# First matrix product of batches 4 to 15: a seven-product scheme replaced by three passes over 12-bit parts, with a direct projection

## The chip, the cores and the metric

One core of one Trainium2 chip runs the kernel. The metric is the device time of one execution in microseconds, the median over the runs made. The kernel before takes 173.54 us (three runs, 172.73 to 173.70).

## The reference

```python
# x (16, 256, 512), cond (16, 256), W3 (256, 512), W2 (512, 512), weight and rram (512, 512), all float32
q_emb = relu(cond @ W3 + b3)                           # (16, 512)
v_sum = sum(x, axis=1, keepdims=True)
h = relu(((256 * x + v_sum) * q_emb[:, None, :]) @ W2 + b2)
x_q = where(h > 0.33, 0.5, where(h < -0.33, -0.5, 0.0))
w_q = where(weight > 0.2, 0.6, where(weight < -0.2, -0.6, 0.0))
return x + einsum('bsd,od->bso', x_q, w_q + rram)
```

The first product ends in a comparison: of `h` only the side of 0.33 on which it lies is kept. The second product (the projection) takes 0 or 1 for each hidden value and a factor 0.5 at the end. The 16 batches of 256 tokens make 4096 tokens, 32 output tiles of 128 tokens by 512 columns.

## The kernel before, in words

Each engine has a list of operations written out by hand, and semaphores order the engines. Nothing is moved by a scheduler: an engine works through its list in order, and an operation behind a waiting one waits too.

Input: SyncE loads x two batches (a "pair") at a time into two slots of `x_in`. VectorE transposes a batch into `xT` in one instruction (`transpose_batch`, L532). The token sum of a batch comes from VectorE (L581, batches 2, 3, 6, 7) or from ScalarE (`accumulate`, L436), and ScalarE scales the batch in four pieces of 128x256 (`scale`, L430). Batches 0 and 1 are handled in finer pieces at the start.

First product: batches 0 to 3 are multiplied directly in float32 by `w2_sb` (L1005, L1010, L1018). Batches 4 to 15 are three groups of four batches. A group is a 2x2 block product of 512-token halves and 256-row halves of W2, done with seven block products instead of eight (`p1` to `p7`, L855 to L927). VectorE makes four sums of x blocks for it (`token_sum_1` to `_4`, L591 to L620), GpSimd four sums of W2 blocks (`s_mix`, L309 to L317), and VectorE adds and compares seven results in PSUM (`c11`, `sum_16`, `sum_167`, `c22`, `c21`, `c12`). Results are kept in `hid`. These matmuls have float32 operands, and each call leaves two records in the trace.

Projection: the weight is quantized (VectorE L748, L750; GpSimd L322, L327), transposed (L729) and split into a rounded high part `wT_hi` (ScalarE L479) and a rest `wT_lo` (GpSimd L331), both of type fp32r. An fp32r matmul leaves one record. Group 0 is projected tile by tile with eight matmuls of 512 columns (`project_part`, L932). Groups 1 to 3 are projected two tiles at a time, again with seven products instead of eight (`project_pair`, L955, 28 matmuls of 256 columns per pair). For that GpSimd makes sums of hidden blocks (`a_sum`) and of weight blocks (`b_sum`, `b_lo`), and finishes part of each output (L370, L376); VectorE adds five or six PSUM pieces per pair (L679 to L716). Tile 3 and the last tile of the last group are projected directly, the last in two column halves.

The order on TensorE is in L1001 to L1070: direct product, group 1's seven products, projection of group 0, then for groups 2 and 3 the seven products followed by the projection of the group before, and at the end the last group's projection.

## Time and profile before

| | |
|---|---|
| runs | 173.70, 172.73, 173.54 us, median 173.54 |
| profiled execution | span 171.1 us from its first to its last instruction; the page gives no other time for it, so what lies around the span is taken as 173.54 - 171.1 = 2.4 us |
| TensorE matmul | 165.2 us busy, 97% |
| VectorE | 131.6 us, 77% |
| GpSimd | 85.4 us, 50% |
| ScalarE | 67.7 us, 40% |
| granted TensorE clock | 1.000 |
| DMA | 28.99 MB, mean 169 GB/s |

Busy time of TensorE overstates its work, since matmuls overlap in the records. The distance from one matmul's start to the next is the price of one; the chain that ended last gives it over long stretches.

### The profile page before, as it was taken

The page shows a single profiled execution, that of the slowest core. Times are in us where ns is not written, and L with a number is a line of the kernel's source. Part 1 is how long each engine was busy: PE and PEld are TensorE (multiplying, and loading weights), DVE is VectorE, ACT ScalarE, POOL GpSimd, SP SyncE. Part 2 cuts the span into 40 slices and gives each one's busy share as a digit, 9 for nine tenths or more (in the row PEclk, how much of TensorE's full clock was granted, in tenths as well). Part 3 has the DMA queues.
Part 4 walks back from the last instruction along what each step waited for, and adds up shares of the span by engine and source line. Part 5 has one row for each costly group of instructions (what it writes and reads, how often), then busy time and mean ns, then how long its engine had stood idle before and what let it go on. Part 6 is the DMA issues. An engine that isn't in the chain of part 4 may idle for free.

```text
span 171.1 us, 2177 instructions
## 1 busy us (share of the span) xinstructions
PE 165.2 (97%) x684; PEld 122.3 (71%) x684; DVE 131.6 (77%) x196; ACT 67.7 (40%) x173; POOL 85.4 (50%) x85
## 2 busy tenths in 40 slices
PE   7989999999899999999999999999999999999991
PEld 2889997777445478687645459997644459999991
DVE  3589997998999997785978878779926167776751
ACT  2154269927202269998109994531000001001000
POOL 3000950659105691560199002758498003999990
PEclk9999999999999999999999999999999999999999
DMA  5999999999700594609949204993293000353166
GB/s 168 223 238 247 234 217 225 219 222 211 137 0 0 129 356 126 124 9 226 377 173 337 107 0 119 329 347 131 82 325 145 0 4 3 121 199 113 66 255 231
DMA packets 31211, 28.99 MB, mean 169 GB/s; under 512 B 1600, under 2 KB 22368, under 8 KB 31200
## 3 DMA queue, kind: packets, MB, share of 16 engines
q1 hardware_dynamic: 30128, 28.07, 60.4%
q10 hardware_dynamic: 1008, 0.79, 1.6%
q8 instruction: 5, 0.08, 0.2%
q14 instruction: 6, 0.05, 0.1%
q0 software_dynamic: 64, 0.00, 0.0%
HBM read 20.47 MB, written 8.39 MB: 169 GB/s over the span
## 4 chain that ended last, share of the span: by engine, by line
PE 92%; issue 1%; DVE 1%; ACT 0%; ACTq 0%
PE out_ps L955 12%; PE hid_ps L955 10%; PE out_ps L932 9%; PE out_ps L1018 8%; PE hid_ps L925 6%; PE hid_ps L883 6%; PE hid_ps L859 6%; PE hid_ps L898 6%; PE hid_ps L906 6%; PE hid_ps L918 6%; PE hid_ps L866 6%; PE hid_ps L1005 5%; PE hid_ps L1010 4%; PE hid_ps L932 2%; ACT xT L430 0%
## 5 line engine op out<-in xcount | busy, mean ns | idle before, releaser
L430 ACT ACTIVATE xT<-xT,coef,q_scale 128x256 f32<-128x256 f32 x64 | 33.9, 592 | 14.0 <-DVE coef L583 7.8
L532 DVE STREAM_TRANSPOSE xT<-x_in 128x1024 f32<-128x1024 f32 x15 | 30.8, 2060 | 0.1
L436 ACT ACTIVATE junk<-xT,q_emb 128x256 bf16<-128x256 f32 x40 | 19.8, 496 | 11.6 <-DVE xT L532 11.4
L370 POOL TENSOR_TENSOR x_res<-x_res,pieces 128x256 f32<-128x256 f32 x8 | 5.9, 734 | 27.3 <-DVE x_res L706 27.3
L486 ACT ACTIVATE pieces<-out_ps 128x256 f32<-128x256 f32 x6 | 2.3, 387 | 32.5 <-PE out_ps L955 29.6
L1018 PE MATMUL out_ps<-xT,w_sb 128*128 128x512 f32 x32 | 14.1, 600 | 0.0
L376 POOL TENSOR_TENSOR x_res<-x_res,pieces 128x256 f32<-128x256 f32 x16 | 13.5, 863 | 0.0
L932 PE MATMUL out_ps<-wT_lo,hid 128*128 128x512 f32 x32 | 13.3, 415 | 0.0
L932 PE MATMUL out_ps<-wT_hi,hid 128*128 128x512 f32 x32 | 12.5, 390 | 0.0
L1018 PEld LDWEIGHTS out_ps<-xT,w_sb 128*128 128x128 f32 x32 | 9.8, 309 | 3.7
L883 PE MATMUL hid_ps<-t_sum,s_mix 128*128 128x512 f32 x24 | 11.4, 595 | 0.7 <-issue 0.7
L925 PE MATMUL hid_ps<-xT,s_mix 128*128 128x512 f32 x24 | 11.5, 601 | 0.0
L898 PE MATMUL hid_ps<-t_sum,s_mix 128*128 128x512 f32 x24 | 11.3, 592 | 0.0
L906 PE MATMUL hid_ps<-t_sum,s_mix 128*128 128x512 f32 x24 | 11.3, 592 | 0.0
L918 PE MATMUL hid_ps<-t_sum,w_sb 128*128 128x512 f32 x24 | 11.3, 592 | 0.0
L859 PE MATMUL hid_ps<-xT,w_sb 128*128 128x512 f32 x24 | 10.9, 597 | 0.0
L866 PE MATMUL hid_ps<-xT,w_sb 128*128 128x512 f32 x24 | 10.8, 592 | 0.0
L359 POOL TENSOR_TENSOR a_sum<-hid 128x1024 fp32r<-128x1024 f32 x2 | 4.7, 2347 | 11.8 <-DVE t_sum L619 11.8
L331 POOL TENSOR_TENSOR wT_lo<-wT,wT_hi 128x1024 fp32r<-128x1024 f32 x2 | 4.7, 2362 | 11.6 <-ACT wT_hi L479 11.6
L918 PEld LDWEIGHTS hid_ps<-t_sum,w_sb 128*128 128x128 f32 x24 | 7.4, 308 | 3.6 <-issue 1.4
L643 DVE SCALAR_TENSOR_TENSOR e<-hid_ps,th_col,e 128x512 f32<-128x512 f32 x6 | 4.4, 734 | 6.9 <-PE hid_ps L906 6.9
L310 POOL TENSOR_TENSOR s_mix<-w_sb 128x256 f32<-128x256 f32 x2 | 2.3, 1150 | 14.5 <-DVE coef L549 14.5
(134 smaller groups left out, 415.8 us busy)
## 6 DMA issues: line engine op xcount, KB each, us to landing
x_in<-in_x SPq DMA_DIRECT2D x24, 256.0 KB, 5.4
x_res<-in_x SPq DMA_DIRECT2D x3, 2048.0 KB, 9.2
out<-x_res SPq DMA_DIRECT2D x24, 256.0 KB, 3.6
x_in<-in_x SPq DMA_DIRECT2D x1, 2048.0 KB, 9.8
out<-x_in SPq DMA_DIRECT2D x7, 256.0 KB, 2.1
x_in<-in_x SPq DMA_DIRECT2D x12, 128.0 KB, 6.5
w_sb<-in_L_cond_W SPq DMA_DIRECT2D x4, 256.0 KB, 6.4
x_res<-in_L_ffn_weight SPq DMA_DIRECT2D x4, 256.0 KB, 7.1
```

Source lines behind the costliest of these rows:

```text
L430: nc.scalar.activation(part, part, ACT.Identity, bias=coef[:, n, k:k + 1], scale=q_scale[:, n, k:k + 1]).then_inc(s_xs, 1)
L532: nc.vector.transpose(xT[:, s, :, cols].rearrange("p j (n t) -> p n j t", t=BLK), x_in[:, p % SLOTS, b * NB:(b + 1) * NB].rearrange("p n ( ...
L859: mm = nc.tensor.matmul(hid_ps[j][:], weight_block(0, 0, j, k), xT[:, g % 2, k, 0:TOK], start=(k == 0), stop=(k == 1))
L866: mm = nc.tensor.matmul(hid_ps[j][:], weight_block(0, 1, j, k), xT[:, g % 2, 2 + k, 0:TOK], start=False, stop=(k == 1), skip_group_check=True)
L883: mm = nc.tensor.matmul(hid_ps[2 - j][:], s_mix[:, 1, j, k], t_sum[:, 1, k], start=(k == 0), stop=(k == 1))
L898: mm = nc.tensor.matmul(hid_ps[3 - j][:], s_mix[:, 0, j, k], t_sum[:, 0, k], start=(k == 0), stop=(k == 1))
L906: mm = nc.tensor.matmul(hid_ps[2 - j][:], s_mix[:, 2, j, k], t_sum[:, 2, k], start=False, stop=(k == 1), skip_group_check=True)
L918: mm = nc.tensor.matmul(hid_ps[0][:], weight_block(1, 1, j, k), t_sum[:, 3, k], start=(k == 0), stop=(k == 1))
L925: mm = nc.tensor.matmul(hid_ps[3 - j][:], s_mix[:, 3, j, k], xT[:, g % 2, 2 + k, TOK:], start=False, stop=(k == 1), skip_group_check=True)
L932: mm = nc.tensor.matmul(bank[:, cols], hid[:, g % 2, k, c * P:(c + 1) * P], w[:, k, cols], start=(k == 0 and w is wT_lo), stop=(k == KD - ...
L955: mm = nc.tensor.matmul(pair_ps[bank][u % 2], hidden[:, k, tokens], w[:, k], start=(start and k == 0 and i == 0), stop=(stop and k == 1 an ...
L1018: mm = nc.tensor.matmul(out_ps[m][:], chunk_columns(w2_sb[:, k], m), xT[:, 0, k, TOK:], start=(k == 0), stop=(k == KD - 1))
```

## The change

Batches 0 to 3 keep their direct float32 product. For batches 4 to 15 the work goes by blocks of two batches (512 tokens; `b` is 2 to 7). Each operand is split into a high part of about 12 bits (`Copy` with the scale `SHRINK = 1 - 2**-13` into an fp32r tile), and a low part, the difference. Instead of the four products of such parts three are made: high by high (with the high weight divided by `CUT = 4096`), a product of the "difference" parts `wk_d` and `xk_d`, and low by low. The result is `(CUT + 1) * main > CUT * cross + threshold`, where `main` holds the first and the third product in one PSUM bank and `cross` the second. All operands are fp32r. Per block that is 4 column blocks of 12 matmuls of 512 columns.

- TensorE: `multiply(b)` for the seven products; every tile is projected by eight matmuls of 512 columns (only the last tile in two halves).
- ScalarE: added are four `w2_round`, four `w2_high`, one `high_part` (128x1024) for each of 12 batches, 24 `bound_of` (128x512 from PSUM). It sums 9 batches instead of 10. Removed are the copies of p1 and of pair pieces and `b_hi`.
- GpSimd: four `wk_l`, four `wk_d`, and `low_part` of batches 4 to 7 (two instructions each) join the weight work (4 + 4 + 1 instructions). After that it has nothing.
- VectorE: `difference` (two instructions of 128x512) for every batch from 4, from batch 8 also the two low-part instructions (`split_rest`), 24 `compare`, 32 tiles of `finish` (the last in halves), one of the two `wT_lo`. The token sums, and the additions of both seven-product schemes, are gone. VectorE sums batches 3, 5, 10, 12 and 14; batches 2, 4, 6, 7, 8, 9, 11, 13 and 15 are summed on ScalarE.

The core of the diff:

```diff
+            def low_part(n):
+                pool.wait_ge(s_xk_h, n - FIRST + 1)
+                for k in range(0, KD, 2):
+                    ks = slice(k, k + 2)
+                    nc.gpsimd.tensor_tensor(part_of(xk_l, n)[:, ks], batch_of(n)[:, ks],
+                                            part_of(xk_h, n)[:, ks].bitcast(F32), ALU.subtract).then_inc(s_xk_l, 1)
...
+            def high_part(n):
+                act.wait_ge(s_xs, XS_DONE[n])
+                if n >= FIRST + 4:
+                    act.wait_ge(s_main, KD * (n // 2 - DIRECT - 1))
+                nc.scalar.activation(part_of(xk_h, n), batch_of(n), ACT.Copy, scale=SHRINK).then_inc(s_xk_h, 1)
...
+            def split_rest(n):
+                difference(n)
+                dve.wait_ge(s_xk_l, 2 * (n - FIRST))
+                for k in range(0, KD, 2):
+                    ks = slice(k, k + 2)
+                    nc.vector.tensor_tensor(part_of(xk_l, n)[:, ks], batch_of(n)[:, ks],
+                                            part_of(xk_h, n)[:, ks].bitcast(F32), ALU.subtract).then_inc(s_xk_l, 1)
+            def difference(n):
+                dve.wait_ge(s_xk_h, n - FIRST + 1)
...
+                for k in range(0, KD, 2):
+                    ks = slice(k, k + 2)
+                    nc.vector.scalar_tensor_tensor(part_of(xk_d, n)[:, ks], part_of(xk_h, n)[:, ks].bitcast(F32),
+                                                   1.0 + 1.0 / CUT, batch_of(n)[:, ks],
+                                                   ALU.mult, ALU.subtract).then_inc(s_xk_d, 1)
+            def compare(b, m):
+                u = KD * (b - DIRECT) + m
+                dve.wait_ge(s_main, u + 1)
+                dve.wait_ge(s_bound, u + 1)
...
+                nc.vector.scalar_tensor_tensor(hid[:, b % 4, m], hid_ps[2 * (u % 2) + 1][:], CUT + 1.0, bound[:, u % 2],
+                                               ALU.mult, ALU.is_gt).then_inc(s_hid, 1)
...
+            def multiply(b):
+                for m in range(KD):
+                    u = KD * (b - DIRECT) + m
+                    cross, main = hid_ps[2 * (u % 2)], hid_ps[2 * (u % 2) + 1]
+                    if u == 0:
+                        pe.wait_ge(s_wk_d, KD)
+                    if u < 2:
+                        pe.wait_ge(s_cls_hid, 2 * u + 2)
+                    else:
+                        pe.wait_ge(s_hid, u - 1)
+                    pe.wait_ge(s_xk_h, 2 * (b - DIRECT + 1))
+                    for k in range(KD):
+                        nc.tensor.matmul(main[:], wk_h[:, m, k], xk_h[:, b % 2, k], start=(k == 0), stop=False)
+                    pe.wait_ge(s_xk_d, 4 * (b - DIRECT + 1))
...
+                    pe.wait_ge(s_xk_l, 4 * (b - DIRECT + 1))
...
+            multiply(2)
+            multiply(3)
             project(0)
             project(1)
+            for b in range(4, BLOCKS):
+                multiply(b)
+                project(b - 2)
+            project(BLOCKS - 2)
+            project(BLOCKS - 1, range(TILES - 1))
```

On TensorE the direct product of batches 2 and 3 (L1018 before, L689 now) is followed before by this (the names in brackets are the semaphores waited for; "direct_hidden_ready" counts VectorE's `quantize`):

```order
L859 MATMUL hid_ps<-xT,w_sb 128x512 [waits direct_hidden_ready,batch_piece_scaled]
L859 MATMUL hid_ps<-xT,w_sb 128x512
L866 MATMUL hid_ps<-xT,w_sb 128x512 [waits p1_copied]
L866 MATMUL hid_ps<-xT,w_sb 128x512
L883 MATMUL hid_ps<-t_sum,s_mix 128x512 [waits direct_hidden_ready,token_sum_ready,weight_sum_ready]
```

and now by this:

```order
L706 MATMUL hid_ps<-xk_h,wk_h 128x512 [waits batch_high_ready,direct_hidden_ready,w2_difference_ready]
L706 MATMUL hid_ps<-xk_h,wk_h 128x512 x3
L709 MATMUL hid_ps<-xk_d,wk_d 128x512 [waits batch_difference_ready]
L709 MATMUL hid_ps<-xk_d,wk_d 128x512 x3
L714 MATMUL hid_ps<-xk_l,wk_l 128x512 [waits batch_low_ready]
L714 MATMUL hid_ps<-xk_l,wk_l 128x512 x3
L706 MATMUL hid_ps<-xk_h,wk_h 128x512 [waits batch_high_ready,direct_hidden_ready]
```

The first column block now needs the high parts of both batches 4 and 5, and two of VectorE's `quantize` of the direct product instead of one; its bank for the second needs four.

On VectorE the stretch from the weight comparison to the first results of the new product was:

```order
L748 TENSOR_SCALAR wT<-x_res 128x2048 [waits weight_loaded]
L750 TENSOR_SCALAR x_res<-x_res 128x2048 [waits weight_compared]
L588 TENSOR_SCALAR hid<-hid_ps,b_col 128x512 [waits direct_product_ready] x4
L532 STREAM_TRANSPOSE xT<-x_in 128x8x4x32 [waits x_in_loaded3]
L581 TENSOR_REDUCE x_sum<-xT 128x4 [waits batch_transposed]
```

and is now:

```order
L558 TENSOR_SCALAR wT<-x_res 128x2048 [waits weight_loaded]
L560 TENSOR_SCALAR x_res<-x_res 128x2048 [waits weight_compared]
L465 STREAM_TRANSPOSE xT<-x_in 128x8x4x32 [waits direct_product_ready,x_in_loaded3]
L530 SCALAR_TENSOR_TENSOR xk_d<-xk_h,xT 128x2x256 [waits w2_low_ready,w2_high_ready,batch_high_ready]
L530 SCALAR_TENSOR_TENSOR xk_d<-xk_h,xT 128x2x256
L530 SCALAR_TENSOR_TENSOR xk_d<-xk_h,xT 128x2x256 [waits w2_low_ready,w2_high_ready,batch_high_ready]
L530 SCALAR_TENSOR_TENSOR xk_d<-xk_h,xT 128x2x256
L537 TENSOR_SCALAR hid<-hid_ps,b_col 128x512 [waits direct_product_ready] x2
L465 STREAM_TRANSPOSE xT<-x_in 128x8x4x32 [waits direct_product_ready,x_in_loaded3]
L537 TENSOR_SCALAR hid<-hid_ps,b_col 128x512 [waits direct_product_ready] x2
```

The four `quantize` (L588, now L537) have moved behind a transpose that waits for a load, and behind four new instructions with two operands each in SBUF; two of them stand behind a second transpose as well.

GpSimd's list from the splits of W2 to its end is now:

```order
L311 TENSOR_TENSOR wk_l<-w_sb,xk_d 128x4x128 [waits w2_rounded] x4
L316 TENSOR_TENSOR wk_d<-wk_h,wk_l 128x4x128 [waits w2_low_ready,w2_high_ready] x4
L288 TENSOR_TENSOR xk_l<-xT,xk_h 128x2x256 [waits batch_high_ready]
L288 TENSOR_TENSOR xk_l<-xT,xk_h 128x2x256
L295 TENSOR_TENSOR x_res<-wT,x_res 128x512 [waits weight_compared] x3
L295 TENSOR_TENSOR x_res<-wT,x_res 128x512 [waits weight_compared]
L301 TENSOR_TENSOR x_res<-x_res 128x512 [waits weight_quantized,rram_loaded] x4
L306 TENSOR_TENSOR wT_lo<-wT,wT_hi 128x4x256 [waits weight_hi_ready]
```

The pair of L288 stands there three times in front of the three L295 (batches 4, 5, 6), and once between them and the last L295 (batch 7); it is shown once.

## Rows read from the trace of the kernel before

**Rows 1.** The page: span, busy time by engine, the granted clock in 40 slices.

```profile
span 171.1 us, 2177 instructions
...
PE 165.2 (97%) x684; PEld 122.3 (71%) x684; DVE 131.6 (77%) x196; ACT 67.7 (40%) x173; POOL 85.4 (50%) x85
...
PEclk9999999999999999999999999999999999999999
```

**Rows 2.** The chain that ended last: start us, us, what.

```profile
24.91 13.95 PE out_ps L1018 x32
38.86 3.43 PE hid_ps L859 x8
...
45.73 0.67 issue
...
48.35 1.72 PE hid_ps L898 x4
...
62.09 7.28 PE out_ps L932 x32
...
105.96 3.36 PE hid_ps L955 x28
...
163.88 3.76 PE hid_ps L932 x24
```

**Rows 3.** Timeline, VectorE, tail: start us, us, engine, line, operation.

```profile
167.67 0.42 DVE L823 SCALAR_TENSOR_TENSOR x_in<-hid_ps,x_in 128x256 f32<-128x256 f32 x1 [0.53 <-PE hid_ps L932]
```

**Rows 4.** Groups by line and shape: busy us, mean ns of one; VectorE.

```profile
L532 DVE STREAM_TRANSPOSE xT<-x_in 128x1024 f32<-128x1024 f32 x15 | 30.8, 2060 | 0.1
L670 DVE SCALAR_TENSOR_TENSOR x_res<-out_ps,x_res 128x512 f32<-128x512 f32 x8 | 5.4, 679 | 3.8 <-PE out_ps L932 3.8
...
L581 DVE TENSOR_REDUCE x_sum<-xT 128x4 f32<-128x1024 f32 x4 | 4.9, 1220 | 0.1
...
L748 DVE TENSOR_SCALAR wT<-x_res 128x2048 f32<-128x2048 f32 x1 | 1.2, 1227 | 1.1 <-DMA x_res<-in_L_ffn_weight 1.1
...
L619 DVE TENSOR_TENSOR t_sum<-xT,t_sum 128x1024 f32<-128x1024 f32 x3 | 3.6, 1215 | 0.0
```

**Rows 5.** The same view, GpSimd and ScalarE.

```profile
L327 POOL TENSOR_TENSOR x_res<-x_res 128x512 f32<-128x512 f32 x4 | 5.0, 1281 | 1.8 <-DMA x_res<-in_L_ffn_rram_variation 1.8
...
L310 POOL TENSOR_TENSOR s_mix<-w_sb 128x256 f32<-128x256 f32 x2 | 2.3, 1150 | 14.5 <-DVE coef L549 14.5
...
L479 ACT CAST wT_hi<-wT 128x1024 fp32r<-128x1024 f32 x2 | 2.1, 1048 | 11.3 <-DVE wT L729 11.3
```

**Rows 6.** Timeline, VectorE and ScalarE: four operations of a kind, and one summed batch.

```profile
26.07 0.51 ACT L436 ACTIVATE junk<-xT,q_emb 128x256 bf16<-128x256 f32 x1
...
28.18 2.08 ACT L430 ACTIVATE xT<-xT,coef,q_scale 128x256 f32<-128x256 f32 x4
...
31.44 2.72 DVE L588 TENSOR_SCALAR hid<-hid_ps,b_col 128x512 fp32r<-128x512 f32 x4
```

**Rows 7.** Tile x_in, last SyncE issue of the fourth pair (window 26.5 to 27.3).

```profile
L231 SPq DMA_DIRECT2D x_in<-in_x x1: 1077/1077/1077, 26.3 to 26.3; - x1
...
DMA to landing us min/median/max: 7.0/7.0/7.0
```

**Rows 8.** Timeline of VectorE and GpSimd, 38 to 45 us.

```profile
39.68 3.75 POOL L327 TENSOR_TENSOR x_res<-x_res 128x512 f32<-128x512 f32 x3
...
42.22 2.28 DVE L596 TENSOR_TENSOR t_sum<-xT 128x1024 f32<-128x1024 f32 x1 [0.51 <-ACT xT L430]
```

**Rows 9.** The same, 116 to 122 us.

```profile
116.42 1.56 DVE L596 TENSOR_TENSOR t_sum<-xT 128x1024 f32<-128x1024 f32 x1
116.86 3.39 POOL L376 TENSOR_TENSOR x_res<-x_res,pieces 128x256 f32<-128x256 f32 x2
...
118.08 1.57 DVE L604 TENSOR_TENSOR t_sum<-xT,t_sum 128x1024 f32<-128x1024 f32 x1
```

**Rows 10.** Timeline, TensorE, the first eight matmuls.

```profile
1.19 3.60 PE L830 MATMUL out_ps<-warm 128*128 128x512 bf16 x8 [1.19 <-DVE warm L732]
```

More of the change, by code:

```diff
@@ L510, in _ @@
[L510 to L518 removed]
+            high_part(7)
+            bound_of(2, 2)
+            bound_of(2, 3)
@@ new lines, in _ @@
+            transpose_batch(6)
+            difference(4)
+            difference(5)
+            quantize(0, 0)
+            quantize(0, 1)
+            transpose_batch(7)
+            quantize(0, 2)
+            quantize(0, 3)
+            difference(6)
+            compare(2, 0)
+            compare(2, 1)
+            quantize(1, 0)
+            difference(7)
+            compare(2, 2)
+            quantize(1, 1)
+            quantize(1, 2)
+            compare(2, 3)
+            quantize(1, 3)
```

917 lines of the change are left out of this document (293 added, 624 removed).

## The prediction

> **What bounds the kernel now.** I read the page first: TensorE is busy 97% of the span at full granted clock, VectorE 77% [rows 1]. Then the chain of waits. It is TensorE from end to end: one line of matmuls follows the other, and the only gap is the 0.67 us in front of L883 at 45.73 [rows 2]. From 38.86, where batches 4 to 15 begin, to the last matmul's end at 163.88 + 3.76 = 167.64 are 128.8 us. Behind it stand 3.5 us: the last addition ends at 168.1 [rows 3], the rest is the last store. So what the change does to TensorE's own work counts one to one, and every other engine counts only where TensorE comes to wait for it. The prices on TensorE, start to start: an fp32r matmul of 512 columns 7.28 / 32 = 0.2275 us, one of 256 columns 3.36 / 28 = 0.120 us, a float32 record 1.72 / 4 = 0.43 us [rows 2].
>
> **TensorE's work.** Removed is all of the 128.8 us. In its place come six blocks of 48 matmuls, 288 x 0.2275 = 65.5 us, 31 tiles of eight, 248 x 0.2275 = 56.4 us, and 16 half-width matmuls of the last tile, 1.9 us. Sum 123.8 us, a gain of 4.9 us, and the old 0.67 us gap is in it. (The first product falls by about 8 us, the projection without its seven-product scheme grows by 3.) The float32 product of batches 0 to 3 stays, and so does the tail.
>
> The Trainium skill ("TensorE: Matmul & The Clock Gate", Back-to-back issue gap) gives N/2.4 + 2.5 ns, which is 216 ns for 512 columns. By it these 536 matmuls would take 6.2 us less than by the row. The row is from this kernel with the same operand type, and the sum keeps it.
>
> **Prices elsewhere.** VectorE: a transposed batch 2.06, a finished tile 0.68, a batch sum 1.22, and an addition of two SBUF tiles 1.215 for 1024 columns, so 0.61 for 512, taken as 0.62 [rows 4]; a `quantize` 2.72 / 4 = 0.67 [rows 6]; `compare` reads PSUM like a finished tile, 0.68. `difference` has two SBUF operands but is of a form that the trace lacks there. From below the nearest row is the one-operand comparison, 1.227 for 2048, 0.31 per 512; from above the finished tile, 0.68. I take 0.62, the row with the same number of SBUF operands. GpSimd: 1.28 for 128x512 [rows 5]. ScalarE: one batch summed and scaled 2.1 + 2.1 = 4.2 [rows 6], a cast of 128x1024 1.05 [rows 5].
>
> One more price is a collision. At 42.22 VectorE starts an addition of two SBUF tiles while GpSimd adds until 39.68 + 3.75 = 43.43; it ends at 44.50, that is 1.07 after GpSimd, though alone it takes 1.2 [rows 8, 4]. It stood for as long as GpSimd's operation ran. It works both ways: among VectorE's two at 116.42 and 118.08, GpSimd's two 256-column additions take 3.39 us [rows 9]. So a pair of such operations on both engines goes one after the other, each waiting for the whole of the other's.
>
> **The waits that the change adds on TensorE.** Each is a meeting of two times.
>
> 1. First column block, 38.9. It needs two `quantize`, which now stand behind a transpose of batch 6 and four `difference`. The fourth pair's last load is issued at 26.3 and lands 7.0 later, at 33.3 [rows 7]; the same bytes are ahead of it, so I leave it there. Transpose to 35.4. ScalarE, free of batch 3 at 26.1 [rows 6], does two `w2_high` (1.3), batch 4 (4.2) and its high part (1.05) to 32.7, then batch 5's scaling and high part to 35.9. GpSimd's low parts of batch 4 pass before VectorE comes, those of batch 5 run from 36.0 against the differences: two of the four wait 1.28 each. 35.4 + 4 x 0.62 + 2 x 1.28 = 40.4, two `quantize` to 41.8, TensorE at 41.9. Wait 3.0.
> 2. Second column block: batch 7's transpose (2.06) and two more `quantize` (1.34) to 45.2, while the first block of 12 x 0.2275 = 2.73 ends at 44.6. Wait 0.6.
> 3. Third: two differences of batch 6 and one collision, 45.2 + 1.24 + 1.28 = 47.7, `compare` to 48.4; asked for at 47.9. Wait 0.5. With a second collision it is 1.8.
> 4. The eighth. ScalarE has batch 7's high part at about 50.6 (transposed 43.9, then 4.2 for sum and scale, two `bound_of` between them, 1.05). GpSimd: two low parts and two collisions to 54.4, one L295 and four L301, 5 x 1.28, to 60.8; transpose of the second weight half to 62.9, `compare` to 63.6. TensorE asks at 48.4 + 5 x 2.73 = 62.1. Wait 1.5.
> 5. The third column block of batches 8 and 9. VectorE has a list from 64.2 (ScalarE's cast of the second half done) to that block's release: `wT_lo` 1.2, four transposes 8.2, three `compare` 2.0, eight finished tiles 5.4, eight split instructions (two `difference` and two low parts for each of batches 8 and 9) 5.0, one sum 1.3, and about 0.7 until ScalarE has batch 8's high part; 23.8 in all, to 88.0. TensorE: from 63.7 the last block 2.73, 64 projection matmuls 14.6, two blocks 5.5, so it asks at 86.5. Wait 1.5. The fourth block comes 0.4 late in the same way (four split instructions and a `compare`, 3.2, against 2.73).
>
> Together 7.5. From then on VectorE's list for a block is two transposes 4.1, eight splits 5.0, four `compare` and four tiles 5.4, a sum 1.3, so 15.8 against TensorE's 80 x 0.2275 = 18.2, with GpSimd idle. What hides VectorE's new work there is those 18.2 us; 2.4 are to spare.
>
> **Sum.** -4.9 + 7.5 = +2.6 on the span of 171.1. The page gives 171.1 for the profiled span and the runs 173.54 as median, 2.4 more, which nothing here touches. 173.54 + 2.6 is 176.1; I say 176.2.
>
> **Bounds of the unknown.** `difference` and split at 0.31 would take 1.2 from wait 1 and all of wait 5, -3.2; at 0.68 they add 1.1. The fp32r matmul with these operands could go at half a float32 record, 0.215, or at 0.240, twice the 256-column price: 288 x 0.0125 is 3.6 us, about half of which comes back as wait, so -1.8 or +1.8. GpSimd's four `wk_l` read W2 in steps of four elements. A strided one of 256 columns took 1.15 [rows 5], so 2.3 instead of 1.28; then the tiny coefficient products of batches 0 and 1, also of two SBUF operands, stand behind them, and TensorE's start is up to 3 late. Below nothing they can't be: at 1.28 they fit.
>
> **The rivals.**
> - *No collision with this form* (ends faster). If `difference` does not wait for GpSimd, VectorE reaches `quantize` at 39.2, wait 1 is 0.4, wait 3 nothing, wait 4 some 0.7; waits 2 and 5 stay. Sum 3.7, -4.9 + 3.7 = -1.2, 172.3. It decides as soon as the four L530 between 35 and 41 last 0.62 each. For it: no row has this form colliding. Against it: rows 8 and 9 show the two-operand addition, and this one reads the same two tiles.
> - *TensorE stays the bound*, all waits gone: 173.54 - 4.9 = 168.6. It needs VectorE's 23.8 us list to be shorter by two as well. Against it: every item has a row.
> - *The clock falls in wait 1.* TensorE idles 3.0 us where it never did for over 0.7. The first eight matmuls, after idling, are 0.43 us apart [rows 10] for 512 columns of one pass, twice 0.2275, though the clock column reads 9 there [rows 1]. If some 16 matmuls after 41.9 ran so, +3.2, 179.4. The Trainium skill (same page, Part 1) has such a fall to 1.2 GHz after idling and a return under load; it would give that same 179.4. No later row shows one.
> - *A late start by the strided splits*: up to 179.
> - *Not what it says*: if the splits cost two records per call, 288 x 0.2 us more, 234. The fp32r projection shows one.
>
> **Chances.** Forecast 0.58 (its own range 174.4 to 178.5), no collision 0.17, TensorE the bound 0.05, clock or late start 0.19, the last 0.01. The range runs from the no-collision case to the two dear ones, 172.2 to 180.0. A measurement of this kernel tells about 0.5% from no change, so faster means under 172.7 and slower above 174.4. Faster: the second rival and over half of the first, 0.16. Same: the rest of the first and the lower edge of the forecast, 0.14. Slower 0.70.
>
> **What would show it.** In the changed profile the chain leaves TensorE: an idle of about 3 us before the first L706 released by VectorE's L537, L530 rows of 1.9 us beside L288 in 35 to 41 us, gaps of 1 to 2 us near 62 and 86 released by L546, and none after 92; matmuls of L706, L709, L714 0.2275 apart; GpSimd silent after 64. Wrong would be L530 at 0.6 throughout, a pitch outside 0.215 to 0.24, or waits for `batch_low_ready`.

## The result, and the profile after

The changed kernel takes 176.53 us (median of 4, 174.63 to 176.92), the kernel before beside it 173.62: ratio 1.0176, 95% interval 1.0114 to 1.0237. It is slower by 2.9 us (by 1.1% to 2.4%); forecast was 2.6. The profiled execution has a span of 175.0 against 171.1, 3.9 more. The page, as in [rows 1]:

```profile
span 175.0 us, 2023 instructions
...
PE 165.0 (94%) x672; PEld 134.3 (77%) x672; DVE 128.0 (73%) x171; ACT 90.0 (51%) x188; POOL 40.1 (23%) x31
...
PEclk9999999999589999999999999999999999999999
```

TensorE computes for as long as before (165.0 us), though it has less to do, and one digit of its clock reads 5. In 46 to 48 it is 0.50 as well and in 48 to 50 0.55; three of the windows (window: length, busy time and count of PE, PEld, DVE, ACT and POOL, granted clock, DMA share, GB/s):

```profile
42.00:44.00 2.00, 0.33 (x1) 0.36 (x2) 2.00 (x4) 1.34 (x2) 0.55 (x1) 0.75 0.66 124
44.00:46.00 2.00, 2.00 (x6) 1.52 (x6) 2.00 (x2) 0.00 (x0) 2.00 (x3) 0.50 0.00 0
...
50.00:52.00 2.00, 2.00 (x10) 1.65 (x9) 0.07 (x1) 1.84 (x5) 0.62 (x1) 1.00 0.68 123
```

TensorE's timeline from the direct product (26.48; it was 24.74 before) over the first new blocks to the eighth (66.71); start, us, engine, line, operation, idle before:

```profile
26.48 14.12 PE L689 MATMUL out_ps<-xT,w_sb 128*128 128x512 f32 x32
43.67 2.04 PE L706 MATMUL hid_ps<-xk_h,wk_h 128*128 128x512 f32 x4 [3.08 <-issue]
...
48.93 1.50 PE L706 MATMUL hid_ps<-xk_h,wk_h 128*128 128x512 f32 x4
50.26 1.07 PE L709 MATMUL hid_ps<-xk_d,wk_d 128*128 128x512 f32 x4
51.17 1.07 PE L714 MATMUL hid_ps<-xk_l,wk_l 128*128 128x512 f32 x4
...
64.77 1.07 PE L714 MATMUL hid_ps<-xk_l,wk_l 128*128 128x512 f32 x4
66.71 1.19 PE L706 MATMUL hid_ps<-xk_h,wk_h 128*128 128x512 f32 x4 [0.87 <-DVE hid L546]
```

The same timeline in batches 8 and 9:

```profile
88.60 1.07 PE L714 MATMUL hid_ps<-xk_l,wk_l 128*128 128x512 f32 x4
90.01 1.21 PE L706 MATMUL hid_ps<-xk_h,wk_h 128*128 128x512 f32 x4 [0.34 <-DVE hid L546]
...
93.06 1.19 PE L706 MATMUL hid_ps<-xk_h,wk_h 128*128 128x512 f32 x4
```

The chain that ended last, where [rows 2] stood:

```profile
10.88 1.44 DVE coef L481
12.45 1.96 DVE q_emb L476
...
60.22 3.80 POOL x_res L301 x3
...
66.71 1.05 PE hid_ps L706 x4
...
150.48 19.95 PE out_ps L720 x88
170.43 1.92 PE hid_ps L720 x16
```

It begins with two operations on 16 numbers per partition or fewer that took 1.44 and 1.96 us ([rows 2] began with TensorE), goes over GpSimd's weight sums to 66.71, and is TensorE's from 90 on. What stood at the two heads of it, first VectorE's timeline:

```profile
15.41 2.05 DVE L465 STREAM_TRANSPOSE xT<-x_in 128x1024 f32<-128x1024 f32 x1
...
35.25 2.10 DVE L465 STREAM_TRANSPOSE xT<-x_in 128x1024 f32<-128x1024 f32 x1 [1.31 <-DMA x_in<-in_x]
37.24 5.01 DVE L530 SCALAR_TENSOR_TENSOR xk_d<-xk_h,xT 128x512 fp32r<-128x512 f32 x4
42.18 1.40 DVE L537 TENSOR_SCALAR hid<-hid_ps,b_col 128x512 fp32r<-128x512 f32 x2
...
66.00 0.65 DVE L546 SCALAR_TENSOR_TENSOR hid<-hid_ps,bound 128x512 fp32r<-128x512 f32 x1
```

And GpSimd's; its first row are the splits of W2 that hold the two small operations, its second meets the differences at 37.24:

```profile
10.19 4.17 POOL L311 TENSOR_TENSOR wk_l<-w_sb,xk_d 128x512 fp32r<-128x512 f32 x2 [7.74 <-ACT xk_d L365]
...
38.28 3.42 POOL L288 TENSOR_TENSOR xk_l<-xT,xk_h 128x512 fp32r<-128x512 f32 x2 [0.53 <-ACT xk_h L361]
```

So TensorE's own end moved from 167.64 to 170.43 + 1.92 = 172.35, by 4.7 us, and this splits up:

| part | us |
|---|---|
| work: 288 + 248 matmuls at 0.2267 (19.95 / 88 in the chain), and 1.92; 123.4 against 128.8 | -5.4 |
| start: direct product at 26.48, was 24.74 | +1.7 |
| wait before 43.67 (its idle is 3.08) | +3.1 |
| clock: 43.67 to 50.26 are 6.6 for four groups that take 0.91 each later | +3.0 |
| eighth block: 64.77 + 0.91 to 66.71 | +1.0 |
| batches 8 and 9: 89.5 to 90.01 and 92.9 to 93.06, and three slower restarts of 0.14 | +1.1 |
| sum (0.2 of the 4.7 has no name) | +4.5 |

Behind TensorE's end stand 2.65 us instead of 3.5, which brings 4.7 to the 3.9 of the span. And the executions differ: three had a mean granted clock of 0.98 (1.00 is 2.4 GHz, 0.50 is 1.2) and spans of 174.4 to 175.1, the fourth 1.00 and 172.8. The profiled one is of the three. (Medians below are over all executions; ratios, and ranges where nothing else is said, leave out those over 1.5% above the fastest of the same kernel.)

### The profile page after: what moved, and what is told of

It reads as the page before. It is cut to its first block, busy times and chain, and to the rows that moved or that the text cites. A ratio compares the mean times of both kernels' runs of the same rounds, so it can differ in the third digit from the quotient of the medians.

```text
span 175.0 us, 2023 instructions
## 1 busy us (share of the span) xinstructions
PE 165.0 (94%) x672; PEld 134.3 (77%) x672; DVE 128.0 (73%) x171; ACT 90.0 (51%) x188; POOL 40.1 (23%) x31
## 4 chain that ended last, share of the span: by engine, by line
PE 48%; DVE 17%; ACT 15%; POOL 8%; issue 7%; DVEq 0%; POOLq 0%; ACTq 0%
PE out_ps L720 24%; PE hid_ps L706 8%; PE hid_ps L709 7%; PE hid_ps L714 7%; ACT xT L344 7%; DVE xT L465 5%; ACT warm L350 5%; POOL x_res L295 3%; POOL xk_l L288 2%; ACT xk_h L361 2%; POOL x_res L301 2%; DVE x_sum L479 2%; DVE coef L481 1%; DVE q_emb L476 1%; ACT wk_h L369 1%
## 5 line engine op out<-in xcount | busy, mean ns | idle before, releaser
L720 PE MATMUL out_ps<-wT_lo,hid 128*128 128x512 f32 x124 | 48.2, 389 | 0.0
L720 PE MATMUL out_ps<-wT_hi,hid 128*128 128x512 f32 x124 | 48.2, 389 | 0.0
L706 PE MATMUL hid_ps<-xk_h,wk_h 128*128 128x512 f32 x96 | 27.5, 409 | 4.3 <-issue 3.1
L720 PEld LDWEIGHTS out_ps<-wT_hi,hid 128*128 128x128 f32 x124 | 23.3, 188 | 4.8
L720 PEld LDWEIGHTS out_ps<-wT_lo,hid 128*128 128x128 f32 x124 | 23.3, 188 | 4.8
L709 PE MATMUL hid_ps<-xk_d,wk_d 128*128 128x512 f32 x96 | 26.5, 399 | 0.0
L714 PE MATMUL hid_ps<-xk_l,wk_l 128*128 128x512 f32 x96 | 26.5, 399 | 0.0
L706 PEld LDWEIGHTS hid_ps<-xk_h,wk_h 128*128 128x128 f32 x96 | 18.6, 198 | 10.0 <-issue 3.8
L530 DVE SCALAR_TENSOR_TENSOR xk_d<-xk_h,xT 128x512 fp32r<-128x512 f32 x24 | 20.4, 895 | 4.3 <-ACT xk_h L361 4.3
L709 PEld LDWEIGHTS hid_ps<-xk_d,wk_d 128*128 128x128 f32 x96 | 18.6, 194 | 4.0
L288 POOL TENSOR_TENSOR xk_l<-xT,xk_h 128x512 fp32r<-128x512 f32 x8 | 12.0, 1519 | 9.6 <-ACT xk_h L361 9.6
L689 PE MATMUL out_ps<-xT,w_sb 128*128 128x512 f32 x32 | 14.1, 599 | 0.0
L689 PEld LDWEIGHTS out_ps<-xT,w_sb 128*128 128x128 f32 x32 | 9.8, 309 | 3.8
## 6 DMA issues: line engine op xcount, KB each, us to landing
x_in<-in_x SPq DMA_DIRECT2D x12, 128.0 KB, 6.0
```

Source lines behind the costliest of these rows:

```text
L530: nc.vector.scalar_tensor_tensor(part_of(xk_d, n)[:, ks], part_of(xk_h, n)[:, ks].bitcast(F32), 1.0 + 1.0 / CUT, batch_of(n)[:, ks], ALU.m ...
L689: mm = nc.tensor.matmul(out_ps[m][:], chunk_columns(w2_sb[:, k], m), xT[:, 1, k], start=(k == 0), stop=(k == KD - 1))
L706: nc.tensor.matmul(main[:], wk_h[:, m, k], xk_h[:, b % 2, k], start=(k == 0), stop=False)
L709: mm = nc.tensor.matmul(cross[:], wk_d[:, m, k], xk_d[:, b % 2, k], start=(k == 0), stop=(k == KD - 1))
L714: mm = nc.tensor.matmul(main[:], wk_l[:, m, k], xk_l[:, b % 2, k], start=False, stop=(k == KD - 1))
L720: mm = nc.tensor.matmul(bank[:, cols], hid[:, b % 4, k, c * P:(c + 1) * P], w[:, k, cols], start=(k == 0 and w is wT_lo), stop=(k == KD - ...
```

## The experiments

Twelve runs were made after the result, of which the fifth is the changed kernel itself. Each is timed beside the kernel before on the same chip, whose median in these calls was 173.0 to 173.6. Line numbers in rows of experiments shift by the lines added.

### 1. The two direct banks drained first

```diff
+            quantize(0, 0)
+            quantize(0, 1)
             transpose_batch(6)
             difference(4)
             difference(5)
-            quantize(0, 0)
-            quantize(0, 1)
-            transpose_batch(7)
             quantize(0, 2)
             quantize(0, 3)
+            transpose_batch(7)
```

> Edit: on VectorE the quantize of the first two banks of batches 0 and 1 goes ahead of the transpose of batch 6, and that of the other two ahead of the transpose of batch 7; the same instructions, in another order. My theory of the changed kernel: the 3.08 us before its first new matmul (L706 at 43.67) are the two quantizes behind transpose 6 and four differences, of which two collided with GpSimd. Then the first L706 starts at 40.7, the cross product waits until the differences end at 42.3 (0.7), the clock stays at 2.4 GHz; but the third column block then waits about 2 us for its first compare behind transpose 7, and the eighth still waits about 1.5 for the compare behind the two weight transposes: most of what the start gains is given back, 175.4 us (174.7 to 176.2). Rival 1: the waits at the start simply add to the time: 171.5 (3.1 of wait and 2 to 3 of clock less). Rival 2: VectorE's list from 35 to 66 us is the bound, its order worth nothing: 176.5.

Measured 174.0 (12 executions, 173.8 to 174.2), ratio 1.0037 [1.0011, 1.0063]. Its profile has the clock at 9 or more tenths in every slice. TensorE's timeline, gaps:

```profile
42.36 1.19 PE L709 MATMUL hid_ps<-xk_d,wk_d 128*128 128x512 f32 x4 [0.82 <-DVE xk_d L530]
...
48.93 1.20 PE L706 MATMUL hid_ps<-xk_h,wk_h 128*128 128x512 f32 x4 [1.73 <-DVE hid L546]
...
64.01 1.19 PE L706 MATMUL hid_ps<-xk_h,wk_h 128*128 128x512 f32 x4 [0.98 <-DVE hid L546]
```

The gaps are where they were expected (41.6 to 42.3, the third block, the eighth). But the time fell by 2.5, not by 1.1: I had counted the fall of the clock as absorbed by the later waits, and it is not. Against the changed kernel's execution with the clock at 1.00 (172.8) the span is 0.5 less: that is what the order alone brings, since 3.08 became 0.82 and 1.73. (Against the two executions at 1.00 of run 5 it is 0.6 to 0.7.)

### 2. Matmuls of zeros in the wait

```diff
+            for i in range(12):
+                mm = nc.tensor.matmul(out_ps[3][:], zeros[:, 0:P], zeros[:], start=False, stop=(i == 11))
+            mm.then_inc(s_cls, 1)
```

> Edit: 12 bf16 matmuls of zeros added to the last direct bank fill most of the 3.08 us in which TensorE waits at 40.6 (some 0.21 us each at 2.4 GHz, 2.5 us). Nothing that is waited for moves. Theory: the granted clock stays at 1.00 in 42 to 50, where the changed kernel had 0.75, 0.50 and 0.55, so the first 13 matmuls come 0.227 apart instead of 0.43 to 0.46 (2.9 us less); then the second and third column blocks wait for VectorE (0.6 and 0.5 to 1.8) and the eighth for 1.5 instead of 1.0: 175.7 us (175.0 to 176.3). Rival 1: the fall of the clock is a plain loss: 173.6. Rival 2: it is wholly hidden, since the eighth block waits for the weight transposes whatever TensorE did before: 176.5, its L706 again at 66.7. Rival 3: the clock falls all the same (it was not the idle time): first L706 groups again at 1.7 to 1.9 us.

Measured 174.86 (10 executions, all from 174.5 to 175.2), ratio 1.0088 [1.0058, 1.0119]. TensorE's timeline, the zeros and the first blocks:

```profile
40.24 2.75 PE L700 MATMUL out_ps<-zeros 128*128 128x512 bf16 x12
43.46 1.17 PE L715 MATMUL hid_ps<-xk_h,wk_h 128*128 128x512 f32 x4 [0.47 <-issue]
...
46.66 1.20 PE L715 MATMUL hid_ps<-xk_h,wk_h 128*128 128x512 f32 x4 [0.19 <-DVE hid L542]
...
49.94 0.50 PE L715 MATMUL hid_ps<-xk_h,wk_h 128*128 128x512 f32 x1 [0.26 <-DVE hid L551]
```

TensorE starts its new work no earlier, yet all ten executions lie where one of the changed kernel's four lay. The chip is not the reason: on the same one, run 4, with 2.94 us of idle at that place, has executions with a lower mean clock. So the fall at this place is made by the idle 3 us, and it costs 1.7 of the 176.5. Of its 3.0 us, 1.3 come back. Most of that is in blocks 2 and 3, which without the fall wait for VectorE: they start 0.37 and 0.42 us after the block before them would end at 0.2267 a matmul, with a restart slower by 0.12 each, 1.0 us in all. The eighth block's wait did not grow (0.76 against 0.87), so the rest has no name.

### 3. GpSimd's low parts after the differences

```diff
                 pool.wait_ge(s_xk_h, n - FIRST + 1)
+                if n < FIRST + 2:
+                    pool.wait_ge(s_xk_d, 4)
```

> Edit: GpSimd's low parts of batches 4 and 5 wait until VectorE's four differences of these batches are done. Theory: the four L530 take 2.5 us instead of 5.01, first L706 at 41.2 to 41.5, but the low part product of the first block (L714) then waits about 2 us for GpSimd (four low parts, 5.1 us, from 39.8); GpSimd's list to the weight sums is later by 1 to 2, and the eighth block's wait grows from 1.0 to 2 or more: 176.3 us (175.3 to 177.5). Rival: the collision alone made the first wait, and its removal brings 2.5 us: 174.0. Rival: no collision, L530 as long as before (5.0) wherever GpSimd stands: 177.5 or more.

Measured 174.29 (174.1 to 175.2), ratio 1.0048 [1.0022, 1.0074]. VectorE's timeline:

```profile
36.83 2.63 DVE L532 SCALAR_TENSOR_TENSOR xk_d<-xk_h,xT 128x512 fp32r<-128x512 f32 x4
```

TensorE's:

```profile
40.88 1.16 PE L708 MATMUL hid_ps<-xk_h,wk_h 128*128 128x512 f32 x4 [0.36 <-issue]
...
44.66 1.20 PE L716 MATMUL hid_ps<-xk_l,wk_l 128*128 128x512 f32 x4 [1.69 <-POOL xk_l L290]
```

The same four differences take 2.63 us instead of 5.01, first L708 (L706 there) at 40.88. The collision is shown, and its price, 2.4 for two. The wait went to the low parts (1.69 at 44.66), and no slice of the clock falls there. Of the 2.2 us less, 1.7 are what run 2 gives for the clock.

### 4. The rounding of W2 moved

```diff
-                if k < 2:
-                    w2_round(k)
-            w2_high(0)
-            w2_high(1)
             for k in range(KD):
                 scale_chunk(1, k)
+            w2_round(0)
+            w2_round(1)
+            w2_high(0)
+            w2_high(1)
```

> Edit: ScalarE rounds and scales the first two chunks of W2 after the scaling of batch 1 instead of between the chunks of batch 0, so that GpSimd's strided low splits (2.12 us each) start at 17.5 instead of 10.19, when VectorE's sixteen-element operations of batch 0 are over. Theory: the two operations that took 1.44 and 1.96 instead of 0.16 and 0.18 are short again, the transpose of batch 1 starts at 12.6 instead of 15.4, loads and all that follows come 1.7 to 1.8 us earlier (landing for transpose 6 at 33.5, last L689 matmul ends at 38.9 to 39.5, first L706 at 42.0): 174.8 us (174.3 to 175.6); part may be lost where coef of batch 3 collides instead (up to 2 on VectorE, which has some slack there). Rival: the start is not added, since the first wait shrinks by as much (the wait at L706 then is 4.8 instead of 3.08): 176.5.

Measured 176.11 (174.5 to 176.4), ratio 1.0117 [1.0061, 1.0173]. The expectation was wrong. VectorE's timeline:

```profile
12.59 2.05 DVE L465 STREAM_TRANSPOSE xT<-x_in 128x1024 f32<-128x1024 f32 x1
...
22.35 2.10 DVE L513 TENSOR_TENSOR coef<-x_sum,q_emb 128x4 f32<-128x4 f32 x1
```

TensorE's:

```profile
26.29 14.12 PE L689 MATMUL out_ps<-xT,w_sb 128*128 128x512 f32 x32 [1.17 <-ACT xT L344]
```

The transpose of batch 1 did start at 12.59. Then the coefficient of batch 3, four numbers per partition, met GpSimd's splits, now one unbroken row from 18.10 to 26.5, and took 2.10. The scaling of batch 3 waits for it, and TensorE's direct product idled 1.17 for that and began at 26.29, where it had been 26.48. The collision had only moved to another small operation; the "slack" that I gave it was not there.

### 5. The changed kernel again

> The changed kernel once more, with nothing edited. Its four executions so far had a span of 175.0, 174.4 and 175.1 us with a mean granted clock of 0.98, and one of 172.8 with 1.00. Theory: after the 3.08 us wait at 40.6 the clock falls in some executions and not in others, and this alone makes two groups of times, about 174.6 (mean clock 1.00) and about 176.5 to 176.9 (0.98). Rival: the clock falls in all, and the spread is noise: one group around 176.5. Rival: the two groups come from something else (loads landing later), with no tie to the clock of each execution.

Measured 176.19 (6 executions), ratio 1.0154 [1.0109, 1.0198]. Two executions at 174.74 and 174.82, mean clock 1.00; four from 176.05 to 176.91, 0.978 to 0.99. With the first four: three of ten at 174.6 to 174.8, seven at 176.1 to 176.9, and the clock tells them apart each time. Run 4, with 2.94 us of wait at that place, parts in the same way: 174.5 and 174.6 at 1.00, 176.0 to 176.4 at 0.99 (and 177.5 at 0.98). The mean says only that the clock fell, not where. In both profiled executions of the changed kernel it fell behind this wait; here the windows of 42 to 48 read 0.85, 0.50 and 0.79.

### 6. The splits of W2 without a stride

```diff
-                nc.gpsimd.tensor_tensor(columns_of(wk_l, k), by_columns(w2_sb[:, k]),
-                                        by_columns(w2_round_sb[:, k].bitcast(F32)), ALU.subtract)
+                nc.gpsimd.tensor_tensor(columns_of(wk_l, k), w2_sb[:, k].rearrange("p (m c) -> p m c", m=KD),
+                                        w2_round_sb[:, k].bitcast(F32).rearrange("p (m c) -> p m c", m=KD), ALU.subtract)
```

> Edit: the four low splits of W2 on GpSimd read it as it lies instead of with a stride of four elements. So the low parts of W2 go to wrong columns and the output differs; the number and the size of the instructions are the same. Theory: each takes 1.26 us instead of 2.12, VectorE's two sixteen-element operations are held for 0.5 and 1.1 instead of 1.44 and 1.96, the transpose of batch 1 starts about 1.5 us earlier, and with it loads, the landing for transpose 6 and all that follows: 1.2 to 1.6 us less than the changed kernel in each of its groups: 175.2 median if the clock falls, 173.3 where it doesn't. Rival: the stride is not what makes it long (it stays near 2.1): no change. Rival: the late start is made up elsewhere, as in the run before where the rounding was moved (span 172.8 at clock 1.00): no change in the time though the splits are shorter.

Measured 174.42 (12 executions), ratio 1.0049 [1.0017, 1.0082]; one execution at 172.2 with a mean clock of 0.998, eleven from 173.9 to 175.7 with 0.98 or 0.99 (the four of them above 175.0 are left out of the ratio). GpSimd's group of the splits (count, busy us, mean ns):

```profile
L311 POOL TENSOR_TENSOR wk_l<-w_sb,xk_d 128x512 fp32r<-128x512 f32 x4 | 5.1, 1280 | 14.2 <-ACT xk_d L365 14.2
```

TensorE's timeline:

```profile
24.94 14.12 PE L689 MATMUL out_ps<-xT,w_sb 128*128 128x512 f32 x32
42.21 1.42 PE L706 MATMUL hid_ps<-xk_h,wk_h 128*128 128x512 f32 x4 [3.15 <-issue]
```

1.28 us instead of 2.12, and TensorE at 24.94 instead of 26.48. The wait behind it stayed (3.15), since the loads it hangs on are issued when VectorE has transposed; so all 1.5 us of start count. Against run 5, on the same chip, 2.6 came off where the clock held (one execution) and 1.9 where it fell (median of eleven against median of four). Between the two profiles TensorE's end moves by 1.9: 1.6 are the start, the rest is mainly a wait of 0.50 at the fifth block that run 5's profile has and this one does not.

### 7. Low parts of batches 8 to 15 on GpSimd

```diff
             weight_low(0)
+            for n in range(FIRST + 4, B):
+                low_part(n)
```

(and the same subtraction taken out of VectorE's `split_rest`)

> Edit: the low parts of batches 8 to 15 go from VectorE to GpSimd, which is idle then (as the changed kernel has it for batches 4 to 7). Theory: VectorE loses sixteen operations of 0.68 us, but each difference and low part now collides where they meet; TensorE waited in this stretch only at 89 to 93 (1.2 us), so at most that can be won, and low parts that take 1.3 to 1.9 each on GpSimd can bring a wait of 1 to 2 at the third group of a block: 176.5 (175.5 to 178.5), no gain. Rival: VectorE's list is the bound of the second half, and is relieved: 175.0 or less. Rival: every meeting costs TensorE: over 179.

Measured 175.25 (174.9 to 176.3), ratio 1.0123 [1.0087, 1.016]: 174.9 to 175.3 at clock 1.00, where the changed kernel has 174.6 to 174.8. The differences, VectorE's group (busy us, mean ns):

```profile
L527 DVE SCALAR_TENSOR_TENSOR xk_d<-xk_h,xT 128x512 fp32r<-128x512 f32 x24 | 29.9, 1289 | 5.0 <-ACT xk_h L363 4.8
```

The low parts, GpSimd's:

```profile
L288 POOL TENSOR_TENSOR xk_l<-xT,xk_h 128x512 fp32r<-128x512 f32 x24 | 39.5, 1668 | 48.9 <-ACT xk_h L363 48.9
```

The mean difference grew from 0.895 to 1.289 us. VectorE lost 16 operations of 0.685 and got 24 x 0.39 = 9.5 us of collisions for them. Its busy time stayed where it was (128.3 us; 128.0 in the changed kernel), so its list was hardly relieved, and nothing was won: TensorE's wait in batches 8 and 9 is still there, 0.48 us. This run therefore does not test whether VectorE's list bounds the second half. That it does not from 90 us on is read from the chain of the changed kernel, which is TensorE's alone there.

### 8. The head in another order

GpSimd, and the list of VectorE from the weight comparison to the transpose of batch 9 (q, c, d, T and W stand for `quantize`, `compare`, `difference`, `transpose_batch` and `transpose_weight`, with the code's arguments):

```diff
+                if n == FIRST + 1:
+                    pool.wait_ge(s_xk_d, 4)
...
+            quantize_weight(0)
             low_part(4)
             low_part(5)
+            quantize_weight(1)
             low_part(6)
-            for i in range(3):
-                quantize_weight(i)
-            low_part(7)
+            quantize_weight(2)
             quantize_weight(3)
+            low_part(7)
...
-T6 d4 d5 q00 q01 T7 q02 q03 d6 c20 c21 q10 d7 c22 q11 q12 c23 q13 c30 W0 W1 c31 weight_low(1) T8 c32 c33 T9
+q00 q01 T6 d4 d5 T7 q02 q03 d6 c20 q10 q11 q12 c21 c22 d7 q13 c23 c30 W0 W1 c31 T8 weight_low(1) c32 c33 T9
```

> Edit: the same instructions in another order on VectorE and GpSimd between 31 and 70 us, and one wait more. VectorE: quantize of two direct banks ahead of transpose 6, the other direct banks and compares each as near to the time at which TensorE asks for them as the list allows. GpSimd: one quarter of the weight quantized before low part 4, low part 5 only after the four differences, the other quarters between low parts 5, 6 and 7, all sums after. Theory: the waits of TensorE in the head (3.08, 0.9 to 1.0 at the eighth block) and the one at batch 8 (0.9) each shrink to 0.8 or less, in all 2.3 to 3 us less than the first reordering (174.0) had: 170.5 us (169.8 to 171.8), below the kernel before. Rival 1: VectorE and GpSimd together are full between 35 and 66, so order only moves the waits: 173.5 to 174.5. Rival 2: a wait of 2 us or more appears at the difference of batch 7 and the clock falls: 174 or more.

Measured 170.79 (170.4 to 172.4), ratio 0.9876 [0.9836, 0.9916]: faster than the kernel before. From 40 us on, the view of waits lists one for TensorE (total, times, longest):

```profile
PE hid_ps L719 <- POOL xk_l L290: 0.4, 1, 0.4
```

With the same instructions and one wait more on GpSimd, the 3.1 + 1.0 + 0.7 us of waiting are gone, so they were order: of VectorE's list, and of which operation of GpSimd met which of VectorE's. Three starts between 46 and 62 us are still 0.1 to 0.3 late, which the view does not list. In this profile the granted clock reads 0.95, 0.50 and 0.70 in the windows from 8 to 14, long before the place of the 3.08 us wait; TensorE's longest idle between its first matmul and there is 0.59.

### 9. On it, W2's parts in W2's own layout

```diff
-                        nc.tensor.matmul(main[:], wk_h[:, m, k], xk_h[:, b % 2, k], start=(k == 0), stop=False)
+                        nc.tensor.matmul(main[:], chunk_columns(wk_h[:, k], m), xk_h[:, b % 2, k], start=(k == 0), stop=False)
```

(`wk_d` and `wk_l` alike; `by_columns` returns its argument)

> Edit, on the reordered kernel (170.79): the three parts of W2 keep W2's own layout, so GpSimd's low splits and ScalarE's scaling read and write it as it lies, and TensorE reads its weights with a stride of four elements, as the direct product does. Theory: GpSimd's splits take 1.26 to 1.28 us instead of 2.12, the start is 1.5 us earlier as in the run with the plain split (L689 from 24.94 instead of 26.48), and the strided weight load (0.309 us in the direct product, where the matmul takes 0.44, against 0.194 contiguous) is long because of its four passes, not of the stride: pitch still 0.2266, 169.4 us (168.8 to 170.2). Rival: the stride makes the load 0.3 us, longer than a matmul of 0.2266, and all 288 matmuls of the first product come 0.3 apart: 21 us more, 190.

Measured 171.08 (170.7 to 171.4), ratio 0.9882 [0.9847, 0.9916]; neither theory. Groups of weight loads by line (busy us, mean ns):

```profile
L711 PEld LDWEIGHTS hid_ps<-xk_h,wk_h 128*128 128x128 f32 x96 | 24.4, 310 | 0.4
...
L725 PEld LDWEIGHTS out_ps<-wT_hi,hid 128*128 128x128 f32 x124 | 23.3, 188 | 4.8
```

TensorE's timeline:

```profile
81.16 1.10 PE L714 MATMUL hid_ps<-xk_d,wk_d 128*128 128x512 f32 x4
82.10 1.10 PE L719 MATMUL hid_ps<-xk_l,wk_l 128*128 128x512 f32 x4
```

The stride does make the load 0.310 us instead of 0.194, so that part of the theory is wrong, and four matmuls take 0.94 instead of 0.906. But a matmul comes every 0.235, not every 0.31: the load mostly overlaps. That is 288 x 0.0083 = 2.4 us. Against it stand a first new matmul at 39.34 instead of 40.23 and, after it, no wait that the view lists (run 8 had 0.4, and late starts of 0.1 to 0.3). The direct product begins 0.7 earlier (25.99 for 26.69), not 1.5: the clock is low in 8 to 14 in this profile too (0.87, 0.50, 0.77), and the product before it begins at 18.53 where the run with the plain split had 17.14. It comes out even: TensorE ends at 166.4 in both profiles, and the medians, 0.3 apart, are in each other's range.

### 10. On it, three quarters of the low product left out

```diff
-                    for k in range(KD):
+                    for k in range(1):
                         mm = nc.tensor.matmul(main[:], wk_l[:, m, k], xk_l[:, b % 2, k], ...)
```

> Edit, on the reordered kernel (170.79): the low product of each column block of batches 4 to 15 is done for one chunk of four; the other three chunks are left out, so 72 of TensorE's matmuls (16.3 us at 0.2266). Everything else stays. Theory: the lists of VectorE and ScalarE stand only 2 to 3 us behind TensorE's 18.1 us for each two batches, so waits for the compare of 1 to 2.4 us come back at nearly each pair of batches up to 13, and the head is bound by VectorE and GpSimd: only 5 to 7 us less, 165 (163 to 167). Rival 1: TensorE alone is the bound, all of it is won: 154.5. Rival 2: VectorE bounds wholly, nothing is won: 170.

Measured 163.35 (two executions), 7.4 us less for 16.3 us of matmuls. TensorE's waits for the compare:

```profile
PE hid_ps L711 <- DVE hid L551: 5.7, 7, 1.9
```

Less than half of it is won. Waits come back at seven places, as said, though smaller. So the prediction's order of bounds is right: TensorE first, the lists of the other engines close behind. (These rows name VectorE's `compare`; that its whole list bounds is not shown by them.)

### 11. Reordered, and the splits spaced out

```diff
                 pool.wait_ge(s_w2_round, k + 1)
+                if k < 2:
+                    pool.wait_ge(s_chunk_coef, KD * (k + 1))
+                elif k == 3:
+                    pool.wait_ge(s_coef, 1)
```

> Edit, on the reordered kernel (170.79): GpSimd's strided low splits of W2 stay as they are (2.12 us), but each starts only where VectorE has long transposes ahead: the first after the coefficients of batch 0, the second after those of batch 1, the fourth after the coefficient of batch 3 (waits on semaphores that VectorE raises anyway). Theory: no small operation of VectorE is held for more than 0.3 us before 24, the transpose of batch 1 starts at 12.6 to 12.8 instead of 15.4 to 15.6, the direct product L694 begins at 24.8 to 25.2 instead of 26.5, and the pitch stays 0.2266: 169.1 us (168.6 to 170.0), the fastest of all. Rival 1: the loads, not VectorE, set when TensorE's first new matmul can start, so the start gained is waited off at the low part or the difference of batches 4 and 5: 170.5. Rival 2: the wait so made is long enough for the clock to fall: 172.

Measured 169.03 (168.5 to 170.2), ratio 0.9746 [0.9708, 0.9784]: the fastest, 2.5% under the kernel before beside it. VectorE's timeline:

```profile
12.72 2.09 DVE L474 STREAM_TRANSPOSE xT<-x_in 128x1024 f32<-128x1024 f32 x1
...
22.31 0.16 DVE L522 TENSOR_TENSOR coef<-x_sum,q_emb 128x4 f32<-128x4 f32 x1
```

TensorE's:

```profile
24.93 13.91 PE L698 MATMUL out_ps<-xT,w_sb 128*128 128x512 f32 x32
...
41.05 1.19 PE L723 MATMUL hid_ps<-xk_l,wk_l 128*128 128x512 f32 x4 [0.38 <-POOL xk_l L290]
```

The splits still take 2.13 us each, but none holds VectorE up before 24; the coefficient that took 2.10 in run 4 takes 0.16.

### 12. The same spacing, on the changed kernel alone

The same four lines.

> Edit, on the changed kernel alone: the same waits for GpSimd's splits of W2 as in the run before, nothing else. Theory: the late start of the changed kernel (1.7 to 1.8 us at L689) is this collision alone, and all of it comes off the time, while the 3.08 us wait and the falls of the clock remain: L689 begins at 24.8 to 25.2, L706 at 41.9 to 42.3, executions with mean clock 1.00 at 173.0, those with 0.98 to 0.99 at 174.7 to 175.1, median near 174.6. Rival: as when the rounding was moved, another small operation is held in its place (the coefficient of batch 3 or 5), and the median stays at 176 or more.

Measured 172.14 (170.6 to 172.9, and one left out at 174.2), ratio 0.9889 [0.9843, 0.9935]. TensorE's timeline:

```profile
24.33 13.91 PE L693 MATMUL out_ps<-xT,w_sb 128*128 128x512 f32 x32
40.77 1.16 PE L710 MATMUL hid_ps<-xk_h,wk_h 128*128 128x512 f32 x4 [2.53 <-issue]
```

Four lines of waiting turn the changed kernel from 1.8% slower to 1.1% faster than before. My expectation of 174.6 was wrong. That is 4 us where I expected 2: the direct product begins 2.15 earlier, the wait behind it is 2.53 instead of 3.08, and in three executions the mean clock is 1.00. Its times don't part as cleanly by the clock as the changed kernel's do (172.0 at 1.00, 172.3 at 0.989), so how much of the 4 is the clock stays open. GpSimd's collisions moved here too: the weight comparison of 2048 elements takes 2.38 us instead of 1.21, off the path.

## Why the prediction was right, step by step

The time is right, 176.2 against 176.53, and the sign. The mechanism is right in its main part: TensorE's work shrinks by about 5 us, and waits behind VectorE's list and its collisions with GpSimd take more than that back. The sum is not the one that I wrote: two terms that I had outside it, as rivals with 0.19 between them, came in together, and several inside were too dear. That these nearly cancel, so that the total fits to 0.3, is luck.

**TensorE's work, -4.9.** It is -5.4, for the pitch is 0.2267 instead of 0.2275. The bounds of 0.215 and 0.240 were not needed. The Trainium skill's 216 ns (same title and section as in the prediction), which it gives for a single matmul by itself, is not reached: wherever weights lie contiguously, four matmuls come in 0.905 to 0.91 us at a granted clock of 1.00.

**Prices elsewhere.** `difference` was said to take 0.62, and four take 2.63 without GpSimd beside them (run 3). The collision holds for this form: 5.01 for four (said: 2.48 + 2.56). *No collision with this form* has fallen. The Trainium skill ("SBUF — State Buffer", SBUF: two separate sides) names an exclusive lock between VectorE and GpSimd, held for a whole instruction, which concerns VectorE's operations in a 2-port mode or with two SBUF inputs; for those with two SBUF inputs the rows agree (5.01 against 2.63).

**Wait 1, 3.0 from 38.9 to 41.9.** Measured 3.08, from 40.6 to 43.67. Its length came out of load, transpose, differences, collisions and `quantize` as said, each 1.75 to 2 us later. (The view gives "issue" as what ended it; VectorE's second `quantize` ends at 42.18 + 1.40 = 43.58, and TensorE starts at 43.67.) Run 1 shows that it is the order of the list, run 3 that two collisions are 2.4 of it.

**The late start by the strided splits** stood as a bound ("up to 3 late", 2.3 for a split) and as part of a rival with 0.19. It happened: 2.12 each, 1.7 us late. That is the step of the sum which failed: it used 1.28, the price of reading in a row, although the nearest row to a strided split was the strided one (1.15 for 256 columns), and it had only been given the bound. Also, I had named only products of two operands as those that stand behind them; the 1.96 at 12.45 has one SBUF operand and constants. Run 4 moved the splits onto another small product and won nothing; runs 11 and 12 moved them beside transposes and won all of it. The Trainium skill ("GPSIMD Engine Reference", Performance pitfalls for Q7 kernels) has it that reading SBUF with steps over 8 bytes costs half as much again. Here, with steps of 16 bytes, it is 2.12 against 1.28, two thirds more.

**The clock falls in wait 1.** As a rival I gave it +3.2, from 0.43 per matmul for some 16 of them. It is 0.43 to 0.46 for thirteen or so, 3.0 us at the place. At the end of the kernel it is 1.7 (run 2, run 5), in 7 of 10 executions. The Trainium skill ("TensorE: Matmul & The Clock Gate", Part 1) has the fall to 1.2 GHz after idling and the return under load: the rows 0.75, 0.50, 0.50, 0.55 and then 1.00 agree. In these runs the same program falls in one execution and not in the next.

**Waits 2 and 3, 1.1.** They are gone in the profiled execution: blocks at 1.2 GHz came so late that VectorE was ahead. Where the clock is kept they are there, 0.19 and 0.26 in run 2 (0.37 and 0.42 by starts), smaller than said. This is most of how 3.0 of clock became 1.7.

**Wait 4, 1.5**: 1.0, by the path named (GpSimd's list, second weight transpose to 66.0, `compare`). **Wait 5, 1.9**: 0.7 and 0.4 for restarts; VectorE's list came out at 22.8 us (67.19 to 89.96) instead of 23.8. It was added up from durations; two finished tiles last 1.29 but the next operation starts 1.21 after them, and a transpose lasts 2.00 but the next starts 1.93 after it; over the list that makes the difference. I should have taken starts, as for TensorE.

**The tail** was taken as unchanged and is 0.85 shorter.

So against the forecast's +2.6: start +1.7 and clock +1.7 to 3.0 were not in it; waits 2 to 5 were worth 2.1, not 4.5 (1.1 + 1.5 + 1.9); the work 0.5 more; the tail 0.9. Where the clock holds, the kernel takes 174.6 to 174.8, 1.0 to 1.7 us more than the median of the kernel before beside it.

## What to carry to other kernels

When work moves to engines beside the one that bounds, price the small operations on the path, not only the large ones: two of 16 numbers and less, held behind a strided subtraction on GpSimd, cost more than the eighth block's wait. Where TensorE is made to wait, count the wait twice: once for its length and once, as a risk (here seven executions in ten), for the clock after it; filling it with matmuls of zeros brought 1.7 us back, and where it was divided into shorter ones (runs 1 and 3) no slice of the profile shows a fall. And before giving up a rewrite that loses, look at whether its waits are work or order: the same instructions in another order took 5.4 us less on the same chip, and a place for four splits some 2 more.
